# TensorE given matmuls of the identity in six of its early waits

## The reference

```python
x = x + 0.5 * ffn(layernorm(x))
x = x + attention(layernorm(x))
x = x + 0.5 * ffn(layernorm(x))
```

## Time and profile before

| | us |
|---|---|
| median of 3 runs | 813.4 |
| the 3 runs | 809.28, 813.4, 1249.24 |
| the profiled execution | 810.09 |
| its span, first to last instruction | 808.0 |
| PE busy in the span | 694.0 (86%) |
| DVE busy | 560.2 (69%) |
| ACT busy | 499.7 (62%) |
| POOL busy | 454.8 (56%) |
| mean granted clock of TensorE | 0.955 |

### The profile page before, as it was taken

The page is one execution under the profiler, slowest core; times in us unless marked ns, Lnnn a source line. Parts: engine busy times, 40 slices in busy tenths (PEclk is TensorE's granted clock), DMA queues, the critical chain, the costliest instruction groups (busy, mean ns, idle before and its releaser), DMA issues.

```text
span 808.0 us, 17361 instructions
## 1 busy us (share of the span) xinstructions
PE 694.0 (86%) x4608; PEld 428.6 (53%) x4608; DVE 560.2 (69%) x1596; ACT 499.7 (62%) x973; POOL 454.8 (56%) x545
## 2 busy tenths in 40 slices
...
PEclk9975698999999999999999999999999999999997
...
GB/s 338 425 224 129 134 202 180 143 143 148 153 208 147 151 162 154 196 165 200 189 173 198 152 195 135 150 193 166 176 128 189 177 189 163 152 142 216 231 289 294
DMA packets 321781, 151.52 MB, mean 188 GB/s; under 512 B 302301, under 2 KB 305757, under 8 KB 320925
## 3 DMA queue, kind: packets, MB, share of 16 engines
...
...
## 4 chain that ended last, share of the span: by engine, by line
PE 39%; DMA 11%; DVE 9%; SPq 7%; issue 6%; POOL 5%; ACT 5%; another core or an unknown queue 0%; POOLq 0%; ACTq 0%; DVEq 0%
PE B L1231 22%; PE B L1243 12%; SPq L1061 2%; DMA yt<-t_W,t_idx 2%; PE B L1256 2%; DMA t_W<-t_W 2%; DMA t_ph<-t_p 2%; SPq L1101 2%; SPq L1045 2%; DVE t_th L1730 1%; DMA t_gh<-t_gp 1%; POOL yt L1001 1%; POOL hs L953 1%; PE B L1295 1%; DVE t_gp L1736 1%
## 5 line engine op out<-in xcount | busy, mean ns | idle before, releaser
L1231 PE MATMUL B<-t_W,t_ht 128*128 x1704 | 398.4, 382 | 22.4 <-ACT t_th L1364 5.7
L1231 PEld LDWEIGHTS B<-t_W,t_ht 128*128 128x128 f16 x1704 | 166.5, 98 | 200.5 <-issue 37.4
L1730 DVE SCALAR_TENSOR_TENSOR t_th<-B,t_K,t_th 128x512 f32<-128x512 f32 x142 | 105.9, 747 | 133.0 <-PE B L1231 76.7
L1243 PE MATMUL B<-t_W,t_gh 128*128 x1284 | 160.3, 276 | 8.8 <-issue 3.5
L1001 POOL DMA_INDIRECT yt<-t_W,t_idx x107 | 111.1, 1038 | 96.0 <-ACT t_W L1380 57.4
L953 POOL DMA_INDIRECT hs<-t_s,t_POS x112 | 117.9, 1053 | 58.4 <-issue 30.8
L1243 PEld LDWEIGHTS B<-t_W,t_gh 128*128 128x128 f16 x1284 | 126.0, 99 | 45.2 <-issue 13.4
L1364 ACT ACTIVATE t_th<-B,t_K 128x512 f32<-128x512 f32 x142 | 96.6, 682 | 67.4 <-PE B L1231 42.3
L993 POOL DMA_DIRECT2D t_idx<-hs x142 | 80.6, 571 | 43.3 <-DMA yt<-t_W,t_idx 29.4
L1373 ACT ACTIVATE t_gp<-t_th 128x512 f16<-128x512 f32 x107 | 66.3, 623 | 44.0 <-DVE t_th L1730 35.3
L1736 DVE TENSOR_TENSOR t_gp<-t_th,t_gp 128x512 f16<-128x512 f32 x107 | 75.4, 710 | 16.8 <-ACT t_gp L1373 15.5
...
## 6 DMA issues: line engine op xcount, KB each, us to landing
...
t_ht<-hs SPq DMA_TRANSPOSE x142
t_idx<-hs POOLq DMA_DIRECT2D x142, 0.5 KB
...
```

The source lines that it names most:

```text
L1231: t = eng.matmul(B[b][:], HT[n % HTR][:, (2 * hl + db) * 128:(2 * hl + db) * 128 + 128], W16[:, bass.ds(expert[n] * 4096 + (db * 2048 + wl ...
L1243: t = eng.matmul(B[b][:, 0:256], GH[n % LAG][:, gl, fb * 128:fb * 128 + 128], W16[:, bass.ds(expert[n] * 2048 + (W2OFF + wl * 1024 + fb * ...
L1730: eng.scalar_tensor_tensor(out=th[:], in0=B[b1][:], scalar=K[:, 7:8], in1=th[:], op0=ALU.mult, op1=ALU.mult).then_inc(free[b1], 1)
```

## The change

A new stage `keep(i)`, i from 0 to 25, is put into `ORDER` at six places. It is PE's alone: eight matmuls of 128 columns, the identity with itself, into a bank of the pool `work`. Nobody reads the result, and the stage gives the bank back itself. It waits for the count `free[b]` of its bank like any other user, and stages 7 to 14 also wait for `wl(12)`, the 13th low half. The order of all other stages stays.

| keeps | matmuls | place on PE |
|---|---|---|
| 0 to 6 | 56 | after `sum(9)`, before `rank(0, 1)` |
| 7 to 14 | 64 | after `scale(2)`, before `up(0, 0)` |
| 15, 16 | 16 | after `up(3, 1)`, before `up(4, 0)` |
| 17, 18 | 16 | before `up(4, 1)` |
| 19 to 22 | 32 | after `up(5, 0)`, before `down(0)` |
| 23 to 25 | 24 | after `up(8, 1)`, before `down(5)` |

The test in `table_for` is written in another way as well. `PARTS` has the entries (0, 8) for L = 0 and (0, 16) and (0, 24) for L = 1; with them both forms give the same table for every tile.

Of the string `ORDER`, only the lines up to the last new character are shown; the lines behind them are wrapped anew and have the same characters.

```diff
@@ -103,6 +103,7 @@
 LAG = 4
 NF = 4
+KEEP = 26
 HTR = 4
...
-    "turn", ";": "up", "<": "veil", "=": "wh", ">": "which", "?": "wl", "[": "zero", "~": "ids", "_": "places", "^": "mark", "|": "fill", "}": "spare"}
+    "turn", ";": "up", "<": "veil", "=": "wh", ">": "which", "?": "wl", "[": "zero", "~": "ids", "_": "places", "^": "mark", "`": "keep", "|": "fill", "}": "spare"}
...
-    "))Bt))%Bfzt%(eY)Y)BfeYKYLK$L$KLKL$$)))B)t%feqxw+tY+pK%vYsfLDKL+$+$!!eYYB-t%+KLKL+!^!f!e+^^^$$+++qxwY!pV++++)++++"
-    "+)BYt!!)z)=B=?++>++=?%=:t_?v?!!:fe$$+YY=u?=?=%?^=W=f^!e__!!!)?)?B^==!::W$$YqY:$?u:t?xwp=?^==v%!1!1!1f$?se=?z=^^Y"
-    "??Y==?=??=WW::;;>.$!1N$qx~w~~=!S;;>.;.WNWpv^!PD-;N?[^?>;;>;=S~S!!u.!1!1!1?PP;>N^==;|}Q!1?!1.y1|?S~~V^^E;F>.hhWQW"
-    "PNNSShQEF;;EPQQF!1!1~|_P.uNSP^!!>EF;E|Q*hW~~~.;>;;>FE.*NNSW;;>.NSSWWF~*W~~_;;>;ucP.*~~~~;QEN*PSQ._~*~~NWF~a*S>;_"
...
+    "))Bt))%Bfzt%(eY)Y)BfeYKYLK$L$KLKL$$)))B)t%feqxw+tY+pK%vYsfLDKL+$+$!!eYYB-t%+KLKL+!^!f!e+^^^$$+++qxwY!```````pV++"
+    "++)+++++)BYt!!)z)=B=?++>++=?%=:t_?v?!!:fe$$+YY=u?=?=%?^=W=f^!e__!!!)?)?B^==!::W$$YqY:$?u:t?xwp=?^==v%!1!1!1f$?se"
+    "=?z=^^Y??Y==?=??=WW::````````;;>.$!1N$qx~w~~=!S;;>.;.WNWpv^!PD-;N?[^?>;;>``;=S~S!!u.!1!1!1?PP``;>N^==;|}Q!1?!1.y"
+    "1|?S~~V^^````E;F>.hhWQWPNNSShQEF;;EPQQF!1!1~|_P.uNSP^!!>EF;E|Q*hW~~~.;>;;>F```E.*NNSW;;>.NSSWWF~*W~~_;;>;ucP.*~~"
...
@@ -218,7 +219,7 @@
 def table_for(L, j):
 
     for k, t in enumerate(KNOWN[L]):
-        if t == NT or any(not whole and p <= t and j < 2 * p - 7 for whole, p in PARTS[L]):
+        if t == NT or any(not whole and p == t and j < 2 * t - 7 for whole, p in PARTS[L]):
             return k
 
 
@@ -279,6 +280,10 @@
     def sums():
         for k in range(24):
             yield Want("sum", (k,))
+
+    def keeps():
+        for i in range(KEEP):
+            yield Want("keep", (i,), (("flip", (0, 0)),) + ((("wl", (12,)),) if 7 <= i < 15 else ()), ((("kb", i), work, ("keep", i), 1),), (("kb", i),))
 
     def scales():
         yield Want("scale", (0,), takes=((("scale", 0), bank[0], "scale", 1),), gives=(("scale", 0),))
@@ -564,7 +569,7 @@
         for n in range(N):
             yield tile("put", (n,), (("evict", (n,)), ("ids", (n,))))
 
-    P.run([prepare(), final(), first_routers(), tables(0), tables(1), sums(), scales(), split(), split2(),
+    P.run([prepare(), final(), first_routers(), tables(0), tables(1), sums(), keeps(), scales(), split(), split2(),
            scalars(), rows(), loads(), place(), idents(), whiches(), ups(), downs(), tanhs(), gates(), highs(), glows(), turned(),
            evicts(), puts()])
     return P, seq
@@ -1168,6 +1173,15 @@
                                        stop=k in (15, 23) and h == 7)
                     if k in (15, 23):
                         t.then_inc(s_abs, 1)
+                elif kind == "keep":
+                    b, turn, _ = use["kb", key[0]]
+                    e.wait_ge(s_cast, N_CAST)
+                    e.wait_ge(free[b], turn)
+                    if 7 <= key[0] < 15:
+                        e.wait_ge(s_wl, nth("wl", 12))
+                    for h in range(8):
+                        t = eng.matmul(B[b][:, 0:128], identh[:], identh[:], start=True, stop=True)
+                    t.then_inc(free[b], 1)
                 elif kind == "flip":
                     n, h = key
                     b, turn, _ = use["tb", n, h]
```

More of the change, by code:

```diff
@@ L131 @@
[L131 to L140, removed]
```

40 lines of the change are left out of this document (25 added, 15 removed).

## The result

The changed kernel takes 817.06 us (median of 20 runs, 811.32 to 827.83), the kernel before 812.43 (median of 20 runs, 807.76 to 820.11 but for one of 1249.24). The ratio is 1.0062, 95% interval 1.0040 to 1.0084: slower by 0.6%, where 808.9 us had been forecast. The ratio leaves out the slow runs, those more than 1.5% above the fastest of their kernel (two of each). The profiled execution takes 816.8 us with a span of 815.2, against 810.09 and 808.0 before.

A forecast was written before the change was run, and what follows sets the result against it. All engines wait at `scale(1)`, then POOL's chain up to `put(0)` sets the pace. Only keeps 0 to 6 count: 810.1 - 2.5 = 807.6 us, expected median 808.9; range 803 to 815, forecast chance 0.48.

The forecast's parts named there:

- the first place: Keeps 0 to 6 before `rank(0, 1)`: hidden in idle time, sums at full clock, scale(1) 2.5 us earlier.
- the forecast clock: PE's clock at 40 to 50 us, 0.59 before, expected near 1.0 with keeps 0 to 6.
- rival (a): At `scale(1)`: its answer doesn't move, so nothing is gained; time 810.1, median 811.4 us; chance 0.18.
- The 1.8 us between PE's matmul and DVE: From PE's matmul at 52.79 to DVE at 54.62: cause unknown, taken as a fixed length, keeping the gain at 2.5 us.
- The two pauses of 0.6 us in the sums: In PE's sums at 46.47 and 47.20: about 0.6 us each, cause not named, kept unchanged in the forecast.
- Keeps 7 to 14: Before `up(0, 0)`, all in one bank: 1.1 us a stage cold, 0.67 warm, about 2 us late, costed at nothing.
- Keeps 15 to 22: Before `up(4, 0)`, `up(4, 1)` and `down(0)`: 0.46 us each in PE's slack, value 0 as POOL sets `down(5)`.
- Keeps 23 to 25: Before `down(5)`: 1.4 us within a wait, no cost; possible clock gain of 1.7 us, counted as 0.
- After 150 us: From 150 us on PE is busy all the time, so only the first 150 us can change.
- (c): Keeps 7 to 14 in one bank: at 1.7 us a stage POOL is 5.8 us late, time 813.4 us; chance 0.08.
- (d): Idle pauses between keeps let the clock fall; the first place costs 1.7 us, time 811.8 us; chance 0.07.
- (e): Matmul spacing at full clock is 82 ns, not 57; the 48 sums gain 1.2 us, time 808.9; chance 0.02.

The follow-up runs named there:

- B: A chip of the follow-up runs, whose traces hold about 17,260 engine signals; the kernel before took 804.5 and 802.3 us there in two sets.
- C: A chip of the follow-up runs, of the kind of B by its traces; the kernel before took 804.2 us there.
- D: A chip of the follow-up runs, of the kind of B by its traces; the kernel before took 803.3 us there.
- A: A chip of the follow-up runs, whose traces lack a third of the signals; the kernel before took 813.2 us there.
- Silent keeps: Changed kernel with plain copies for DMA transposes, keeps without bank waits or signals; all 26: 790.64 and 788.52 us on B, 790.41 on C, 791.62 on D.
- v0: Changed kernel without any keeps, DMA transposes replaced by plain copies, on chip B: 786.08 us, 0.9809 of the kernel before.
- t0: Changed kernel without any keeps, DMA transposes replaced by plain copies, on chip A: 796.43 us, 0.9780 of the kernel before.
- 52 wide matmuls: Changed kernel with plain copies for DMA transposes, each keep two matmuls of 512 columns, waits and signals kept: 787.34 us on C, 787.38 on D.
- micro kernel: Only the loads of tokens and weights left, PE running 100 keeps in two banks by turns, on a fifth chip: 46.82 us for 800 matmuls.

## Why the prediction was wrong

**The step that failed is the first place**: that keeps 0 to 6 alternate between two free banks, end at 43.3 and so cost nothing and bring 2.5 us. A bank that a keep has used isn't free when its matmuls end but when its return is back at PE, and that took 8.1 us here: PE stood 7.30 us in front of keep 2. The text had a price for a wait of PE for itself (0.67 to 1.1 us a stage, at most 1.7) but set it only in place 2, where all keeps have one bank. In place 1 every keep from the third on waits for itself as well, two stages back. The step is -2.5 us by the forecast and +5.1 by the trace, and with it falls the forecast clock (0.67 instead of near 1.0 at 40 to 50 us).

That a keep's own work isn't what takes so long is shown on B, C and D: there the same seven keeps run in one row, 3.29 us. What holds PE up in the trace after and on A isn't shown. It may be a late signal, or something that stops PE's issue altogether: on A with place 1 alone the keeps themselves came one by one (46.28 instead of 40.14 for the end of keep 1), and the returns of two banks come together each time. Silent keeps on a chip of A's kind would decide between them, and there is no such run. What the traces show is a set of things that go together: a third of the signals unrecorded, single matmuls 0.7 to 1.4 us apart from 40 us on, own bank returns up to 12 us late, and a kernel before that takes 813 instead of 803 us. The Trainium skill, "NOTIFIC — the notification-queue block", section 7.1 (Overflow: three behaviours, one of which stalls the engine), states that the block that writes the trace's records, when its queue is full, drops the new record, overwrites the oldest, or stalls the engine that makes them. That would tie the missing records to the stalls, but no run here shows it. What the Trainium skill's page "Perfetto Trace Analysis" states under Tensor Engine Instruction, that the signal leaves only once PSUM has acknowledged all bytes, gives an order and no time; the rows have 0.04 us on B (PE's `scale(1)` ends at 48.15, DVE starts at 48.19) and 8.1 after.

**What bounds the kernel: right for the kernel before on its chip, and no more.** All engines stood at `scale(1)`, and it moved everything up to `put(0)`, by 5.1 us the wrong way. On B it doesn't: POOL's scatter ends ACT's wait, 2.67 us were gained on PE and 0 passed on. That is rival (a), by another way than given there. The 1.8 us between PE's matmul and DVE that couldn't be priced is no fixed length: it is 0.04 us in v0 and in the trace after, and 1.3 us in t0 (52.80 to 54.11). It looks like the same hold-up. The two pauses of 0.6 us in the sums are not there on B either.

**Keeps 7 to 14: the price was right in sum.** 1.1 us a stage at 1.2 GHz was given and 8.8 / 8 = 1.1 measured, in part by luck: the last stages ran at full clock, where 0.67 us was given, and took 1.46 (0.84 idle and 0.62). The text took a clock that rises halfway, so `up(0, 0)` was 3.2 us behind the shift of 5.1 instead of 2. ACT's marks of 102.98 came at 110.17, 7.2 us later and so 2.1 more than the shift, inside the 2.5 us of slack that the text gave them: POOL has no pause there. Priced at nothing, it cost nothing.

**Keeps 15 to 22: the second step that failed.** They were to take 0.46 us each and to be worth 0, since POOL sets the time of `down(5)`. PE waited 1.70, 2.36 and 1.19 us for their banks, `down(0)` came 10.9 us late, and ACT's mark, which stands behind the downs' evictions, held up POOL by 1.2 us. Without transposes on A it was more: 7.50 us at keep 17 and `down(5)` at 154.2 against 143.1.

**Keeps 23 to 25** kept the clock up as hoped, 1.00 instead of 0.83, in front of a `down(5)` that was 6.8 us late. They held it up by 0.5 us and brought 1.4 back (5.4 us behind from 147.7 on); the text had named 1.7 and counted 0.

**After 150 us** the text let nothing change, since PE is busy all the time. That is a third failure. In the trace after, PE's distance from the kernel before goes from 5.4 to 1.15 us and to 7 or 8. On B, C and D a short gap near 333 us grows, and the clock falls behind it, in some executions again near 423 and 455. Seven of eight executions lost 2.9 to 7.5 us between 320 and 500 us, about what the keeps cost on these chips, and with 52 wide matmuls the medians are 3.7 and 2.7 us lower. Why 88 small matmuls at 100 to 131 us lengthen a gap at 333 us stays open past the later issue of the transfer. In the profiled execution after, too, the clock fell once between 150 and 700 us, at 466.7, and the kernel before had one such fall, at 222.7.

**The rivals.** (c) had the sign and, with 813.4 us, came nearest to the time, through the wait of PE for itself. But it set that wait in the place where the price was right, so its nearness is luck. (d) was right that idle time lets the clock fall. (e) is refuted: (4.29 - 0.22) / 71 = 57 ns. The Trainium skill's 81 ns ("TensorE: Matmul & The Clock Gate", Back-to-back issue gap) isn't borne out by any stream of this case: 57 here, 58.5 in the micro kernel.
